# Four half tiles of the next block's input projection ahead of a recurrent step's second group of products, instead of two or three

## The reference

```python
def cell(h, x):
    gi = x @ W_ih + b_ih
    gh = h @ W_hh + b_hh
    i_r, i_z, i_n = jnp.split(gi, 3, axis=-1)
    h_r, h_z, h_n = jnp.split(gh, 3, axis=-1)
    r = jax.nn.sigmoid(i_r + h_r)
    z = jax.nn.sigmoid(i_z + h_z)
    n = jnp.tanh(i_n + r * h_n)
    h_new = (1.0 - z) * n + z * h
    return (h_new, h_new)
...
_, hs = jax.lax.scan(cell, initial_state, xs)
...
rw, selected_experts = jax.lax.top_k(routing_weights, TOP_K)
...
for e in range(N_EXPERTS):
    out = out + combine[:, e, None] * (x @ Wa[e] @ Wb[e])
```

## Time and profile before

| what | value |
|---|---|
| time, median of 3 executions | 9652.54 us (9650.1 to 9655.25) |
| the profiled execution, its time | 9647.02 us |
| its span, first to last instruction | 9645.2 us |
| TensorE matmul busy | 9563.8 us (99%) |
| VectorE busy | 5881.8 us (61%) |
| ScalarE busy | 1204.8 us (12%) |
| mean granted TensorE clock | 0.999 |

### The profile page before, as it was taken

How to read it: one execution, slowest core, us unless ns; L and a number is a source line. 1 busy time by engine, 2 the same in 40 slices (tenths; PEclk the granted TensorE clock), 3 DMA queues, 4 the chain that set the end, 5 groups by cost and what they waited for, 6 DMA issues and landing times.

```text
span 9645.2 us, 543927 instructions
## 1 busy us (share of the span) xinstructions
PE 9563.8 (99%) x246424; PEld 6869.9 (71%) x246424; DVE 5881.8 (61%) x30339; ACT 1204.8 (12%) x4955; POOL 492.2 (5%) x1142
## 2 busy tenths in 40 slices
PE   7999999999999999999999999999999999999999
PEld 4666767776676676777768786776778667777687
DVE  5666666666666666666666666656665666656664
ACT  2111111111111111111111111111111111111111
POOL 1000000000000000000000000000000000000100
PEclk9999999999999999999999999999999999999999
DMA  7232222222222223333333333333333333333343
GB/s 191 83 89 64 62 68 62 62 61 64 65 64 65 56 68 80 83 77 79 74 83 83 78 78 76 83 82 79 80 73 84 78 82 80 75 79 80 85 100 91
DMA packets 1229102, 759.53 MB, mean 79 GB/s; under 512 B 850512, under 2 KB 1024080, under 8 KB 1226768
## 3 DMA queue, kind: packets, MB, share of 16 engines
q1 hardware_dynamic: 1202448, 646.76, 27.5%
q0 software_dynamic: 24336, 77.98, 3.5%
HBM read 566.37 MB, written 184.88 MB: 78 GB/s over the span
## 4 chain that ended last, share of the span: by engine, by line
PE 97%; DVE 1%; SPq 1%; DMA 1%; issue 0%; ACT 0%; DVEq 0%
PE gh_ps L1321 81%; PE gi_ps L1372 11%; PE gi_ps L1343 1%; PE y_ps L1412 1%; PE y_ps L1425 1%; SPq L410 1%; PE route_ps L1385 1%; DMA projection<-in_L_cond_W_ih 1%; PE gh_ps L1503 0%; DVE gh L941 0%; PE gi_ps L1425 0%; DMA projection<-w_ih_sums 0%; PE gi_ps L1412 0%; SPq L416 0%; PE gi_ps L1489 0%
## 5 line engine op out<-in xcount | busy, mean ns | idle before, releaser
L1321 PE MATMUL gh_ps<-w_hh_parts,h_parts 128*12 128x288 bf16 (+1 forms) x196608 | 8367.7, 326 | 22.4 <-issue 11.7
L1321 PEld LDWEIGHTS gh_ps<-w_hh_parts,h_parts 128*12 128x12 bf16 x196608 | 5433.8, 88 | 2344.2 <-issue 83.8
L941 DVE STREAM_TRANSPOSE gh<-gh_ps 128x288 f32<-128x288 f32 (+1 forms) x2048 | 1197.5, 585 | 2103.8 <-PE gh_ps L1321 2060.3
L1372 PE MATMUL gi_ps<-projection 128*32 128x128 f32 x37632 | 1354.7, 273 | 1.9 <-DMA projection<-w_ih_sums 1.7
L1237 ACT ACTIVATE gate<-pre 128x24 f32<-128x24 f32 (+1 forms) x2048 | 471.1, 230 | 6965.2 <-DVE pre L954 6965.2
L1372 PEld LDWEIGHTS gi_ps<-projection 128*32 128x32 f32 x37632 | 1114.7, 110 | 276.7 <-DMA projection<-w_ih_sums 3.5
L947 DVE TENSOR_REDUCE gh_sum<-gh 128x36 f32<-128x108 f32 (+1 forms) x2048 | 650.8, 318 | 71.1
L962 DVE TENSOR_TENSOR h_cand<-h_cand,gate 128x12 f32<-128x12 f32 (+1 forms) x2048 | 360.9, 176 | 433.1 <-ACT gate L1237 432.9
L1240 ACT ACTIVATE cand<-h_cand 128x12 f32<-128x12 f32 (+1 forms) x2048 | 442.1, 216 | 930.1 <-DVE h_cand L965 930.1
L974 DVE TENSOR_TENSOR zn<-one_minus_z,cand 128x12 f32<-128x12 f32 (+1 forms) x2048 | 360.2, 176 | 245.7 <-ACT cand L1240 4.5
L987 DVE TENSOR_TENSOR h_parts<-shared,h_parts 128x12 bf16<-128x12 f32 (+1 forms) x2048 | 359.5, 176 | 216.7 <-DVE shared L982 5.0
(11 more groups left out here) (158 smaller groups left out, 2274.5 us busy)
## 6 DMA issues: line engine op xcount, KB each, us to landing
projection<-w_ih_sums SPq DMA_DIRECT2D x672, 256.0 KB, 3.0
projection<-w_ih_by_partition SPq DMA_DIRECT2D x504, 256.0 KB, 2.9
gi_scratch<-gi_stage SPq DMA_DIRECT2D x384, 128.0 KB, 2.9
gi<-gi_scratch SPq DMA_DIRECT2D x256, 192.0 KB, 4.3
shared<-wa_by_partition SPq DMA_DIRECT2D x58, 512.0 KB, 4.2
expert_b<-in_L_ffn_Wb SPq DMA_DIRECT2D x58, 512.0 KB, 4.6
x_raw<-expert_rows_of_h SPq DMA_DIRECT2D x228, 128.0 KB
projection<-in_L_cond_W_ih SPq DMA_DIRECT2D x192, 128.0 KB, 3.8
```

Of the source, the lines that this page charges most:

```text
L941: nc.vector.transpose(gh[k][:, :, :, :], ps[k][sp_][:, 0:GATES * n * Q].rearrange("p (q c i) -> p q c i", q=GATES, i=Q))\
L1321: ins = nc.tensor.matmul(ps[k_out][t % 2][j * Q:j * Q + SPLIT * B, 0:GATES * (o1 - o0) * Q], h_parts[:, (t - 1) % 2, c, :, :].rearrange("p ...
L1372: ins = nc.tensor.matmul(ps_i[(pair + BANK[s]) % 2][j * Q:(j + 1) * Q, 0:COLS // 2], w_half[q % WH][:, c, j * Q:(j + 1) * Q], x_of[what][: ...
```

## The change

`quarter_schedule` gives steps 2 to 61 of a block other ranges. Before, `tiles[0]` had two or three half tiles and `tiles[1]` three. After, `tiles[0]` has four and `tiles[1]` one or two. The number in a step, five or six, is unchanged, and so are steps 0 (0 and 3), 1 (1 and 3), 62 and 63 (none). All five engines' programs read the table, so the copies, sums, loads and stores move with the half tiles.

```diff
 def quarter_schedule(steps, tiles):

     rest = tiles - 7 - 5 * (steps - 4)
-    counts = [(0, 3), (1, 3)] + [(2 + (t * rest // (steps - 4) > (t - 1) * rest // (steps - 4)), 3)
+    counts = [(0, 3), (1, 3)] + [(4, 1 + (t * rest // (steps - 4) > (t - 1) * rest // (steps - 4)))
                                  for t in range(1, steps - 3)]
     counts += [(0, 0)] * 2
     assert sum(a + b for a, b in counts) == tiles
```

## The result

The changed kernel takes 9705.92 us (median of 5, 9695.68 to 9709.34) against 9652.53 us: the ratio is 1.0054, 95% interval 1.0043 to 1.0066. It is 53 us slower. The profiled execution took 9709.34 us, with a span of 9707.4. (Two executions of the kernel before, in the second group of experiments, ran at a granted clock of 0.58 and 0.63 and took 16267 and 26584 us; its median there is that of the others.)

The account below looks back on a forecast made before the run. The prediction took TensorE's rate to bound the kernel, VectorE's chain just fitting under it. Late first-half weight loads and smaller terms summed to 15 us on the median 9652.5, giving 9668 us; range 9651 to 9706.

Parts of the forecast that it names:

- rival 1: Late weight loads of the recurrence are paid in full, nothing absorbed: price 52 us, so 9705 us; chance 0.2.
- the first half's margin: VectorE's first half of h has 0.33 us to spare, 0.24 in every fourth step; cuts are 0.22 or 0.44.
- fourth steps and step 32: Uncovered (4, 1) steps numbered in multiples of four: 80 at 0.08 us, 6.4 us; step 32's extra wait adds 1.0 us.
- plain steps: Uncovered (4, 1) steps not multiples of four: 259, late by 0.11 us, nearly all forgiven, 0.01 each, 2.6 us.
- step 62: In blocks 1 to 5, its wait for the second half of h grows by 0.22 us each: 1.1 us.
- held-up steps: Tight, uncovered steps where VectorE is held up anyway: 12 first halves at 0.44 less 0.10 us, 4.1 us.
- the 0.10 us that a late weight load is forgiven: Recurrence weight loads run one group ahead of their matmuls, so lateness costs only what exceeds about 0.10 us.
- the DMA term: Half product loads on SP's queue: same number, eight half tiles ahead, more than a step to land; cost nothing.
- Rival 3: Seven products a block start as tiles[0]'s fourth half tile; banks VectorE empties may not be free: 15 us more, 9683; chance 0.1.

Follow-up runs that it names:

- the second group of experiments: The three follow-up kernels after the first four, sharing runs of the kernel before, whose median there was 9651.11 us.
- the two ways of removing them: Against the changed kernel: step 36 at (3, 2) instead of (4, 1), 9666.96 us; or SP issuing step 35's product load before the window's store, 9666.54 us.
- step 36 mended: The changed kernel with step 36 of a block at (3, 2) instead of (4, 1): 9666.96 us, ratio 1.0016.

## Why the prediction was right, and where it was wrong

The range and the direction hold the result. The forecast of 9668 us does not: it was 38 us short, and the range reached 9706 us for the sake of rival 1, which did not happen. That 9705.92 lies within it, by 0.1 us, is luck: the direction and the first half's share were foreseen, and most of the loss was not.

**Right: the first half's margin.** With late weights removed, the change costs 15.4 to 15.8 us over its group's kernel before (the two ways of removing them), where the sum had 15. By terms, from the trace of the changed kernel: fourth steps and step 32 at 7.4, measured 7.7; plain steps 2.6, measured 2.3; step 62 at 1.1, measured 1.0; held-up steps 4.1, measured 6.7 in the changed kernel and 4.9 with step 36 mended. The last was an assumption of shares, and these steps also hold some short waits for weights (3.4 us for `w_ih_sums`).

**Right: the 0.10 us that a late weight load is forgiven.** It rested on one event. Cut less margin less 0.11 gives 8.89 and 8.98 us for plain and fourth steps with two moved, and 9.11 and 9.20 with three. Measured are 8.90 and 8.96, 9.11 and 9.18, and no loss with one moved. With nothing forgiven plain steps would take 9.00 and 9.22.

**Wrong: rival 1**, and with it, for this kernel, the Trainium skill's rule (TensorE: Matmul & The Clock Gate, The mechanism) that a weight load overlaps matmuls in flight "only when row_grp differs". Here loads over all 128 rows run a group ahead of their matmuls, 0.11 us, in the traces of both kernels, and the kernel spends that before it loses time. The same section also names a background weight buffer, into which a load can be pulled ahead; that would fit, but no run here shows which buffer a load takes.

**Wrong: the DMA term, "Nothing".** The step that failed reads: "each half product is still loaded when the third before it has ended, eight half tiles ahead [...] with more than a step to land". Half tiles are no measure of time. In the trace of the kernel before, no product starts less than 12.2 us after the end of the third before it. With four half tiles in `tiles[0]`, 14 products of a block start as the fourth of them, and seven of these (steps 9, 17, 25, 36, 44, 52 and 60) have only 9.4 us at the least, because they come before the second group of products and not behind it. That is still more than a step. But the load is not issued when its buffer is free, but when SP gets to it, and I had not asked what else stands on SP's queue in those steps. In one of the seven, step 36, it is the window's store, its wait and its reload: from the issue 1.7 to 3.4 us were left, and the load took 4.0 to 6.3. The term put at nothing cost 31.0 us of waits, and 9.9 more by the clock behind them.

**Rival 3** named these seven starts but expected the bank's release by VectorE to be what is late. Such a wait does not stand among the matmuls' waits of the changed kernel. What waits there is the weights.

**Missing: the clock.** Waits of 2.1 to 3.1 us were followed by half the granted clock in six blocks, 9.9 us together. No rival had it.

No version beats the kernel before by more than a measurement tells.

## What to carry to other kernels

When work is moved ahead in an engine's order, measure the distance from each transfer's release to its first use in time, with the long groups between them, not in units of the work moved; and read what stands before the transfer on the issuing queue in just that step. A single step in 64 can hold most of the loss, so compare steps with like steps and look for the one that stands out, before a small cost is multiplied into a large one. A forecast whose range is saved by a rival that the experiments refute has not been confirmed.

## What the runs showed of the hardware

A weight load that is released late costs matmul time only beyond its lead over its matmuls: 0.11 us behind a group with 128 columns. Beyond it the load and the matmul start together (2255.38 and 2255.39). The load starts 0.05 us after the recorded end of the VectorE instruction that it waited for.

TensorE's granted clock fell to 0.50 behind some of the waits, as in block 1 after 1067.9, and it was back at 1.00 some 4 us later. In the changed kernel six waits of 2.1 to 3.1 us lost it, seven of 0.9 to 1.8 us kept it, and so did block 13 with 3.2 us. With step 36 alone changed, two of 2.3 and 2.5 us lost it and twelve of 0.3 to 1.8 us kept it. With three half tiles moved, all 13 waits of 3.5 to 5.4 us lost it. Why block 13 kept it stays open.

A 256 KB load that lands 3.0 us after its issue in the median took 4.0 to 6.3 us at step 36, behind the window's reload of 512 KB on the same queue; in the kernel before, at the same place, it took 3.7 to 5.6 us.
